# Three unrolled Python loops of an adaLN block kernel written as hardware loops

## The reference, cut to what matters

```python
mod = (silu(c) @ wmod).reshape(1, 6, 1, -1);  sa, ca, ga, sb, cb, gb = ...
h = layernorm(x) * (1 + ca) + sa              # x: 1 x 4096 x 256
x = x + ga * attn(h)   # norm, project, conv, silu, state scan of 16 states over 4096 steps, gate, project
h = layernorm(x) * (1 + cb) + sb
x = x + gb * ffn(h)

# ffn, per token: a softmax router over 16 experts, w; then
q, k, v = [einsum('ne,neh->nh', w, einsum('nc,ech->neh', x, p)) for p in (q_proj, k_proj, v_proj)]
o = softmax(q @ k.T / sqrt(128)) @ v          # 4096 x 4096 scores
out = einsum('enh,ehc->nc', einsum('ne,nh->enh', w, o), o_proj)
```

## Time and profile before

| | |
|---|---|
| three runs | 1463.23, 1463.74, 1466.2 us, median 1463.74 |
| profiled execution | 1463.74 us, of which the span is 1462.0 |
| PE busy | 1381.4 us (94%) |
| DVE, ACT, POOL busy | 1152.2, 679.0, 714.0 us |
| instructions that ran | 20853 |
| instruction transfers | 54 packets with 0.88 MB and 54 with 0.44 MB |

### The profile page before, as it was taken

How to read it: one execution, slowest core, us unless ns; L and a number is a source line. 1 busy time by engine, 2 the same in 40 slices (tenths; PEclk the granted TensorE clock), 3 DMA queues, 4 the chain that set the end, 5 groups by cost and what they waited for, 6 DMA issues and landing times. The chain is left out here.

```text
span 1462.0 us, 20853 instructions
## 1 busy us (share of the span) xinstructions
PE 1381.4 (94%) x6880; PEld 1212.9 (83%) x6880; DVE 1152.2 (79%) x2185; ACT 679.0 (46%) x1345; POOL 714.0 (49%) x633
## 2 busy tenths in 40 slices
PE   5578999999999999999999899999999999999997
PEld 3458989999999999999999777878787878878775
DVE  5758586785876868767667688989999999999865
ACT  3340221302213022130001189888888888888983
POOL 3221131301313113121014167888888898989897
PEclk8688999999999999999999989999999999999998
DMA  4230110011100111000126440010100000000000
GB/s 136 71 97 15 31 38 27 26 39 30 38 27 26 38 30 38 27 26 24 52 84 204 134 152 15 8 37 9 37 8 22 24 15 29 15 30 15 15 15 22
DMA packets 84668, 63.24 MB, mean 43 GB/s; under 512 B 15520, under 2 KB 77392, under 8 KB 84304
## 3 DMA queue, kind: packets, MB, share of 16 engines
q1 hardware_dynamic: 56656, 46.69, 10.2%
q10 hardware_dynamic: 27904, 15.21, 3.6%
HBM read 36.72 MB, written 25.17 MB: 42 GB/s over the span
## 5 line engine op out<-in xcount | busy, mean ns | idle before, releaser
L1425 PE MATMUL ps<-w_hi,memory_r 128*128 128x384 f32 x2048 | 568.0, 343 | 5.8 <-DVE w_lo L858 2.8
L1217 DVE SCALAR_TENSOR_TENSOR wst<-ps,w_cur,wst 128x384 f32<-128x384 f32 x480 | 294.8, 614 | 175.0 <-PE ps L1425 163.6
L1425 PEld LDWEIGHTS ps<-w_hi,memory_r 128*128 128x128 f32 x2048 | 376.0, 189 | 9.9 <-DVE w_lo L858 2.9
L1643 POOL TENSOR_TENSOR memory_rest<-memory_rest,pf 128x512 f32<-128x512 f32 x248 | 346.5, 1397 | 65.9 <-ACT pf L1745 57.5
L1425 PE MATMUL ps<-w_lo,memory_r 128*128 128x384 f32 x1024 | 344.4, 336 | 0.0
L1810 DVE TENSOR_TENSOR p_lo<-pf,p_hi 128x512 fp32r<-128x512 f32 x256 | 282.4, 1103 | 38.3 <-ACT p_hi L1747 37.1
L1425 PEld LDWEIGHTS ps<-w_lo,memory_r 128*128 128x128 f32 x1024 | 194.0, 189 | 4.7 <-issue 1.4
L1745 ACT ACTIVATE pf<-ps 128x512 f32<-128x512 f32 x256 | 153.2, 598 | 70.4 <-PE ps L1917 63.4
L1705 ACT COPY ps<-shift_rows 128x512 f32<-128x512 f32 x256 | 152.8, 597 | 5.9
L1747 ACT ACTIVATE p_hi<-ps 128x512 fp32r<-128x512 f32 x256 | 152.0, 594 | 0.0
L1792 DVE TENSOR_REDUCE mx<-ps 128x1 f32<-128x512 f32 x224 | 147.5, 678 | 1.2 <-PE ps L1908 1.2
(11 more groups left out here) (213 smaller groups left out, 2112.4 us busy)
## 6 DMA issues: line engine op xcount, KB each, us to landing
qk_scratch<-wst ACTq DMA_DIRECT2D x56, 128.0 KB, 2.2
memory<-in_x SPq DMA_DIRECT2D x8, 512.0 KB, 4.1
x_scratch<-memory SPq DMA_DIRECT2D x8, 512.0 KB, 2.9
o_scratch<-memory_rest SPq DMA_DIRECT2D x16, 256.0 KB, 3.0
x2b<-x_scratch SPq DMA_DIRECT2D x32, 128.0 KB, 2.2
out_x<-memory_rest SPq DMA_DIRECT2D x32, 128.0 KB, 1.7
v_scratch<-wst ACTq DMA_DIRECT2D x60, 64.0 KB, 1.8
memory_r<-qk_scratch SPq DMA_DIRECT2D x9, 256.0 KB, 4.4
```

What stands on the lines that cost most here:

```text
L1217: nc.vector.scalar_tensor_tensor(out=dst, in0=src, scalar=w, in1=dst, op0=ALU.mult, op1=ALU.add).then_inc(moe_acc, 1)
L1425: ins = nc.tensor.matmul(ps[:, s % MOE_BANKS, 0:H3], x_part[p][:, k, rows], w_part[:, k, e].rearrange("p t h -> p (t h)"), start=(k == 0 a ...
L1643: nc.gpsimd.tensor_tensor(p_sum[:, p], p_sum[:, p], pf[:, j % PB], ALU.add).then_inc(p_summed, 1)
```

## The change

In `slots` and in `cycle`, and in SyncE's list of output transfers, the Python `for` over i = 1, 2 becomes a hardware loop, `eng.Fori(1, 3)`: blocks 2 and 3 (i = 1) and blocks 4 and 5 (i = 2) run the same instructions, and i is a register. Blocks 0, 1, 6 and 7 stay written out. Each of the five engines has its own loop in each stage, and nothing joins the loops of different engines but the semaphores that were there before.

```diff
@@ slots
         body(0, 1, 2)
-        for i in range(1, NB // 2 - 1):
+        with eng.Fori(1, NB // 2 - 1) as i:
             body(i, 0, 2)
             body(i, 1, 2)
@@ output transfers on SyncE
-                for i in range(1, NB // 2 - 1):
+                with sp.Fori(1, NB // 2 - 1) as i:
                     outputs(i, 0)
                     outputs(i, 1)
```

## The result

The kernel after takes 1484.64 us (median of 4 runs, 1482.84 to 1485.33) against 1463.49 us before (4 runs, 1463.02 to 1466.2): a ratio of 1.0134, 95% interval 1.012 to 1.0147, so 1.2% to 1.5% slower, +21.2 us. The forecast was 1470.3 us with a range to 1484; the sign was right, the size was a third of what came.

The account below looks back on a forecast made before the run. PE was taken as the bound, busy 1381.4 of 1462.0 us. Added costs of 1.3 + 0.8 + 1.9 + 2.6 = 6.6 us gave a span of 1468.6 and, with 1.7 around it, 1470.3 us; 8-in-10 range 1464.5 to 1484.

Parts of the forecast that it names:

- What bounds the kernel, what goes away: Whole kernel: PE is nearly full in touched blocks; executed work and transfers stay, saved instruction transfers are worth nothing.
- f: Touched blocks, every engine: assumed sequencer time of one register instruction, 0.08 us.
- PE's register work at nothing: PE in both stages: its sequencer runs about 3 us ahead, hiding its register instructions; cost nothing, up to 49 us uncovered.
- Scan rounds: Expert stage: 8 rounds where PE waits for DVE each gain two register instructions, 0.16 us; 1.3 us in all.
- Block starts: Attention stage: register instructions on ACT's way to the seed have no slack; 0.2 us a block, 0.8 us in all.
- Inside a block, ACT at nothing "in that slack": Attention turns: a late score delays ACT's exponential by 0.24 us, absorbed by its 0.39 us free a turn; cost nothing.
- T: Both jumps back: assumed time to fetch a loop body's instructions after a taken branch, 3.0 us, range 1.6 to 4.4.
- (B): Rival, both jumps back: jumps cost almost nothing and register work hides; not slower, 1464.2 to 1465.9 us; chance 0.20.
- Expert jump: Expert stage, blocks 3 to 4: DVE's fetch makes its first step 2.2 us late; PE stalls 1.9 us for the carry.
- Attention jump: Attention stage, jump back: ACT's fetch makes the first exponential and seed 2.6 us late; PE stalls for all of it.
- (A): Rival, ACT in the attention stage: register work makes sequencers the bound; 29 us slower, 1493 us; chance 0.15.
- (C): Rival, attention block starts: DVE's `p_lo` overlaps less with POOL, removing PE's 5.2 us wait; faster, 1459 us; chance 0.05.

Follow-up runs that it names:

- regs_pe: Kernel before, blocks written out without loops, block number in a register on PE alone, both stages: 1.0028, +3.9 us.
- regs: Kernel before, touched blocks written out without loops, block number in a register on all five engines: 1.0085, +11.4 us.
- regs_rest: Kernel before, no loops, block number in a register on DVE, ACT, POOL and SP, plain numbers on PE: 1.0047, +6.5 us.
- regs_dve: Kernel before, no loops, block number in a register on DVE alone, both stages: 1.0004, +0.4 us.
- regs_act: Kernel before, no loops, block number in a register on ACT alone, both stages: 1.0038, +4.9 us.
- act_att: Kernel before with one loop only, ACT's in the attention stage: 1.0055, +8.0 us.
- pe_att: Kernel before with one loop only, PE's in the attention stage: 0.9999, no change.
- dve_moe: Kernel before with one loop only, DVE's in the expert stage: 1.002, +2.7 us.
- no_pe: Kernel after without PE's two loops, PE's program written out: 1.0102, +14.3 us over before.
- att_only: Kernel after with loops only in the attention stage (PE, DVE, ACT, POOL); expert stage and SyncE's output list written out: 1.007, +10.0 us over before.
- pe_hint: Kernel after with a prefetch hint only at the head of PE's attention loop body: 1.0124, +16.7 us over before.
- no_act: Kernel after with ACT's attention program written out, all other loops kept: 1.0129, +19.3 us over before.
- hint: Kernel after with a prefetch hint at the head of every loop body: 1.008, +11.2 us over before.
- act_hint: Kernel after with a prefetch hint only at the head of ACT's attention loop body: 1.0133, +20.7 us over before.
- regs_pool: Kernel before, no loops, block number in a register on POOL alone, both stages: 0.9993, -1.9 us.

## Why the prediction was wrong in size

**What bounds the kernel, what goes away.** PE is the bound and nothing was gained, which is right. But time was also lost in places that I hadn't named: before L1361, at the maxima (L1908), and between 678 and 904 us.

**f.** I took 0.08 us; 0.037 to 0.046 was measured. Too high, and yet the touched slots and blocks lost 6.7 us by the numbers where I had 2.1: what was wrong is the places that I costed at nothing, not the price.

**PE's register work at nothing.** Right only for the touched blocks: 0.3 us in the slots and none in the attention blocks (regs_pe). In all this step failed: PE's numbers cost about 3.9 to 4.9 us (the timed regs_pe; regs less regs_rest), more than half of my whole sum. Most of that lies between 678 and 904 us, where PE waits for ACT and for a transfer. Why it does so when PE had numbers in the slots before is open. In after's trace the stretch has only 0.9 us more than in before's.

**Scan rounds, 1.3 us.** Wrong place in the main. A slot has nine rounds (line 940 runs 72 times in before), and I had counted the 8 waits of the earlier trace rows, which are those of the weight loads. Their sum rose from 4.3 to 4.7 us (1.6 + 1.3 + 1.1 + 0.7), while the products' own waits for L940 were shorter before and are gone in after (none is over 0.15 us). Before:

```profile
PE ps L1320 <- DVE scan_b L940: 1.1, 4, 0.5
PE ps L1323 <- DVE scan_a L940: 0.5, 3, 0.2
```

Behind the rounds PE's products of the first touched slot are 0.13 us late in regs and in regs_dve, where I had 0.32. The numbers of DVE and of PE, each alone, brought 0.3 us in the four slots (regs_dve, regs_pe), where all numbers together brought 1.9. ACT's alone brought 0.8 (regs_act), and I had costed ACT in the expert stage at nothing, since it has room (74.73 of 371 us). It has room on average and none ahead of line 735, the router's input: there it computes addresses and issues four transfers in its own order first, and PE now waits for it before L1361, four times, which it did not before. The rest, some 0.5 us, only comes when several engines have registers.

**Block starts, 0.8 us.** Somewhat low: 0.3 to 0.4 us each in PE's start times (the wait for ACT's seed in regs_act grew by (1.7 - 0.6)/2 = 0.55, and by 0.3 in its first block).

**Inside a block, ACT at nothing "in that slack".** This step failed. The blocks lost 4.8 us with no loop at all, 1.2 each, of which the start is 0.3 to 0.4. I had let a late exponential end in ACT's 0.39 us of slack a turn, and in the first half of a block that is what happens: ACT is 0.6 us late and PE loses nothing more from turn to turn. But ACT's lateness goes on to DVE, which has next to none (39.65 of 40 us busy in the middle of a body), and at the last third of the maxima PE waits for it: in regs the products of L1930 are 0.41 us late up to the seventeenth turn of a block and 1.03 at the 24th; the last of a block is 1.33 late. I had looked at the slack of the engine that is delayed and not at that of the one behind it.

**T = 3.0 us.** Right for the bodies that fetched: 2.8 to 3.1 on DVE, ACT and POOL in after (ACT 2.4 in act_att), 3.4 to 3.8 on PE. It was the middle between two transfers of data, so in part luck: in after's stand at the attention jump the trace has one instruction packet of 16 KB from 1139.12 us and three of 8 KB from 1139.57, 1140.18 and 1140.63, each 0.4 to 1.3 us long, and in pe_att, where PE's branch at 1128.4 us took 234 ns, none starts between 1128 and 1140 us. That the small bodies (ACT's 244 and POOL's 86 instructions in the expert stage) jump back in 0.12 to 0.25 us was not foreseen but cost nothing either way. The Trainium skill, "Runtime: NRT & Kernel Launch", section on instruction fetch mechanics, has the rule that a taken branch whose target is outside the window forces a fetch. The runs agree for DVE's and ACT's bodies of 552 to 730 instructions, but POOL's body of 332 fetched too (2.88 us), which is below the 512 that I had worked with. The 108 ns of the Trainium skill, "Advanced Engine Details and Errata", section on control flow timing, on which rival (B) leaned, compare with 0.04 to 0.09 us here for a branch that isn't taken, and with a gap of 0.12 to 0.25 behind a taken one whose body is at hand; by neither could T be known.

**Expert jump, 1.9 us.** Right in place and size: in after PE stands 1.14 us for the carry. It also stands 0.47 us for its own branch, which was longer than its lead and which I had taken as covered; dve_moe alone gave 1.86 at the carry, 2.4 in the ledger.

**Attention jump, 2.6 us.** This is the step that failed by the most at one place: 6.4 + 2.5 - 2.3 (blocks 2 and 3 of regs) = 6.6 us. The stall of 2.6 was right for ACT alone (2.62 in act_att; 2.81 in no_pe, 3.19 in att_only and 3.34 in pe_hint, where more engines have loops). Two things were missing. PE's lead of 3 us, which the earlier trace rows shows in the expert stage, doesn't exist at this place: its sequencer is held at L1930 for `p_lo` until 1138.09 and reaches its branch at 1138.19, so its own 3.77 us are bare. The wait was in the earlier trace rows and I had even counted it as a place without slack, but did not put it together with the lead. And the clock: in every trace in which PE stood 2.6 us or more in this stretch, its products came back at or soon fell to the lower level, 1.2 GHz. In after the granted clock was 0.50 for 10.2 us, and the products of 0.23 us took 0.43. PE was busy 7.49 us of these, half of which is 3.7 us; the step beyond the stall, 6.6 - 3.07 = 3.5 us, is of that size.

**The clock once more.** In slot 2, after ACT's lateness at L1361 (0.29 us), 3.4 us of half clock followed, which makes most of that slot's 2.7. It is in after's and no_act's traces and not in hint's or regs's with a longer wait than after's (0.39 and 0.43 us between the products), nor behind 1.07 us in act_hint at 657.9 us. So a small wait may bring it or not, and I could not tell from the traces what decides.

The account of after's 18.0 us: numbers 1.9 + 4.8, expert jump 1.9, attention jump 6.6, half clock in slot 2 1.7, rest 1.1. The prediction had 2.1, 1.9, 2.6, 0 and 0.

**Rivals.** (A), 1493, came nearer than the forecast, for a wrong reason: ACT's sequencer did not become full, since its lateness doesn't add up from turn to turn. (B) and (C) did not happen. (C)'s mechanism does exist, though: in regs_pool the one wait of 0.9 us for `p_lo` that stands in each block of before is gone in the touched ones, and the trace is 2.6 us shorter. The timed ratio, 0.9993 [0.9984, 1.0002], doesn't prove a gain.

**Open.** Why numbers on PE in the expert stage lengthen the stretch from 678 to 904 us. Why PE's jump in the attention stage is short (0.23 us) where only that stage has loops (att_only, pe_att) and long where the expert stage has them too. Kernels with another alignment of the body were not tried. Also open is what decides whether a half clock follows a wait of well under 1 us, and with it why single traces and timed medians differ by up to 3 us.

## What to carry to other kernels

A loop on an engine's instruction list isn't free even where its engine has room: count the jump back (3 us here for most bodies of 332 to 1180 instructions and 0.1 to 0.25 for those of 86 and 244, unless a prefetch hint stands at the body's head) and look at each engine's lead at that very place, since an engine that was just held by a wait has none. For small delays follow the chain one engine further: the slack that counts is that of the engine that receives the late result. And where a stall of some us would hit TensorE in a dense stretch, add up to about as much again for the clock (1.7 to 3.7 us here). And look behind the blocks that were changed as well: part of the cost of PE's numbers showed only there, and without one kernel with the numbers on PE alone it would have passed for noise.

## What the runs showed of the hardware

- A taken branch to a body that is not at hand: 2.4 to 3.1 us on DVE, ACT and POOL, shown as a gap behind a branch of 0.04 to 0.07 us; 3.3 to 3.8 us on PE, shown as the branch's own duration. With a prefetch hint 0.1 to 0.5 us.
- With the hint no step is left at either jump (hint), for 0.03 to 0.06 us each time it runs.
- With a stall of 2.6 to 3.3 us TensorE's granted clock was 0.50 for 3.4 us (act_att, no_pe), 6.8 us (att_only, pe_hint) or 10.2 us (after, no_act, act_hint). The longest came where PE stood for its own list, with three products between that stall and the wait for `p_lo`. Behind stalls of 1.86 us (dve_moe) and 2.17 us (no_pe) in the expert stage it did not fall.
- Now and then an issue of L756 holds ACT far longer than its neighbours' 0.55 to 0.64 us. In no_act the second issue of one slot took 1.78 us; PE then waited 1.23 us for the router's input and ran 3.4 us at half clock, from 662.4 us. The register in the address doesn't decide it: in after an issue with a fixed address took 1.84 us at 711.8 us, and in regs_pe 1.50 at 706.2.

```profile
654.12 1.78 ACTq L756 DMA_DIRECT2D qk_scratch<-wst  x1
...
659.43 1.74 PE L1361 MATMUL ps<-sn,memory 128*128 128x16 f32 x14 [1.23 <-ACT memory_r L735]
```
